# The order of small steps in the output stage of a decoder layer: clamps, powers and PSUM release

## The reference, cut to what matters

```python
z = out.reshape(B, H, S, dh).transpose(0, 2, 1, 3).reshape(B, S, L)
z = z @ Wo
z = _l2_normalize(z)          # z / max(norm(z), 1e-12)
z = z @ Wff
z = _l2_normalize(z)
z = jax.nn.gelu(z, approximate=False)
...
x = _layernorm(x + z)         # (x - mean) / sqrt(var + 1e-5)
```

## Time and profile before

| | us |
|---|---|
| median of 3 runs | 1892.95 (1890.54 to 1895.87) |
| the profiled execution | 1888.5 |
| its span | 1886.7 |
| PE busy in the span | 1778.7 (94%) |
| ACT busy | 1518.7 (80%) |
| DVE busy | 1444.2 (77%) |
| POOL busy | 669.8 (35%) |
| output stage, from its first matmul to the end of the span | 1886.7 - 1808.87 = 77.8 |

### The profile page before, as it was taken

The page is one execution under the profiler, slowest core; times in us unless marked ns, Lnnn a source line. Parts: engine busy times, 40 slices in busy tenths (PEclk is TensorE's granted clock), DMA queues, the critical chain, the costliest instruction groups (busy, mean ns, idle before and its releaser), DMA issues. The chain is left out here.

```text
span 1886.7 us, 42906 instructions
## 1 busy us (share of the span) xinstructions
PE 1778.7 (94%) x16097; PEld 1195.6 (63%) x16198; DVE 1444.2 (77%) x2682; ACT 1518.7 (80%) x4462; POOL 669.8 (35%) x776
## 2 busy tenths in 40 slices
PE   6999999999999999899999989899999999999985
PEld 5888888888888888659999987622222222222232
DVE  6677777777777777456666655699999999999946
ACT  6777777777777777548898855699999999999964
POOL 2343344433333344405675630022222222222222
PEclk9999999999999999999999999999999999999998
DMA  7222323333333332431101006733453353345001
GB/s 179 46 63 63 63 63 60 61 64 63 57 64 63 61 65 54 106 102 41 45 16 44 18 21 163 203 46 46 62 73 46 46 82 54 46 65 71 1 23 67
DMA packets 139773, 121.61 MB, mean 64 GB/s; under 512 B 78876, under 2 KB 111536, under 8 KB 139568
## 3 DMA queue, kind: packets, MB, share of 16 engines
q1 hardware_dynamic: 139567, 118.88, 32.6%
HBM read 77.29 MB, written 41.53 MB: 63 GB/s over the span
## 5 line engine op out<-in xcount | busy, mean ns | idle before, releaser
L1961 DVE TENSOR_REDUCE s_neg_max<-s_ring 128x1 f32<-128x1024 f32 x512 | 580.7, 1295 | 7.0 <-PE s_ring L1879 6.8
L1921 ACT ACTIVATE s_prob<-s_ring,s_neg_max 128x1024 f32<-128x1024 f32 x512 | 569.8, 1114 | 4.1 <-DVE s_neg_max L1961 2.8
L1892 PE MATMUL s_acc<-s_prob,s_v_norm 128*32 128x256 f32 x4096 | 327.4, 393 | 1.9 <-POOL s_v_norm L1944 1.9
L1879 PE MATMUL s_ring<-f_stack 128*128 128x512 bf16 x923 | 288.5, 386 | 27.2 <-issue 17.6
L1940 POOL TENSOR_TENSOR s_row_inv<-s_row_sum,s_neg_one 128x4 f32<-128x4 f32 x128 | 128.8, 1007 | 410.7 <-ACT s_prob L1921 410.7
L1892 PEld LDWEIGHTS s_acc<-s_prob,s_v_norm 128*32 128x32 f32 x4096 | 81.7, 108 | 218.7 <-issue 215.4
L595 POOL TENSOR_SCALAR a_relu_ring<-a_qT 128x512 f32<-128x512 f32 x64 | 98.6, 1557 | 341.8 <-ACT a_qT L463 314.6
L1879 PEld LDWEIGHTS s_ring<-f_stack 128*128 128x128 bf16 x1024 | 58.5, 97 | 232.7 <-ACT s_prob L1921 221.8
L492 ACT ACTIVATE a_prob<-a_psum,a_neg_max 128x128 f32<-128x128 f32 x512 | 179.5, 400 | 21.4 <-DVE a_neg_max L703 21.4
L746 DVE SCALAR_TENSOR_TENSOR a_att<-a_psum,a_keep_cols,a_num_s 128x128 f32<-128x128 f32 x256 | 72.2, 345 | 133.1 <-ACT a_num_s L518 125.9
L1289 ACT ACTIVATE x_prob<-x_psum,x_neg_max 128x77 f32<-128x77 f32 x512 | 160.6, 337 | 14.1 <-DVE x_neg_max L1445 14.1
(11 more groups left out here) (196 smaller groups left out, 4036.8 us busy)
## 6 DMA issues: line engine op xcount, KB each, us to landing
f_stack<-qk_thirds SPq DMA_DIRECT2D x256, 128.0 KB, 7.4
segment_values<-a_v_stage SPq DMA_DIRECT2D x64, 256.0 KB, 3.2
a_v_pos<-segment_values SPq DMA_DIRECT2D x512, 32.0 KB
qk_thirds<-p_third SPq DMA_DIRECT2D x16, 768.0 KB, 7.7
a_x_in<-in_x_dram SPq DMA_DIRECT2D x16, 256.0 KB, 3.4
a_x_res<-in_x_dram SPq DMA_DIRECT2D x32, 128.0 KB, 2.9
after_attention<-a_normed SPq DMA_DIRECT2D x32, 128.0 KB, 2.4
x_x_in<-after_attention SPq DMA_DIRECT2D x32, 128.0 KB, 2.0
```

The lines of the kernel that those rows point to most:

```text
L1879: last = pe.matmul(ring[n % 3][:, f * HALF:(f + 1) * HALF], k_stack[:, slot, j, kt * P:(kt + 1) * P], q_stack[:, slot, j, f * HALF:(f + 1) ...
L1892: last = pe.matmul(acc[32 * j:32 * j + 32, s], v_norm[:, step // KT % 2, step % 4, j, :], prob[:, step % 4, j, s], start=step % (2 * KT) = ...
L1921: act.activation(prob[:, step % 4, j, :], ring[n % 3][:, :], ACT.Exp, bias=neg_max[:, step % 2, j:j + 1], accum_out=row_sum[:, step % 4, j ...
L1961: dve.tensor_reduce(neg_max[:, step % 2, j:j + 1], ring[n % 3][:, :], AX_X, ALU.max, negate=True).then_inc(max_ready, 1)
```

## The change

TensorE now waits by tile, not by step: tile t waits until the gelu of tile t - 8 has signalled, and every gelu signals. The steps are a list of tile counts, `COUNTS` = seven steps of 4 and two of 2, so the last 512 tokens are two steps. Only one tile of squares of step n + 1 stands ahead of the gelus of step n, not two. On VectorE `residual` is cut: it ends after the statistics, and the rest is `variances`. The order in step n becomes residual(n), clamps(n + 1), normalise(n - 1), factors(n + 1), variances(n); at the end stand residual(8), variances(8), normalise(7), normalise(8). On GpSimd norms(n + 1) comes ahead of deviations(n). Slices and semaphore counts follow the tile counts.

```diff
--- before.py
+++ after.py
@@ -1968,8 +1968,12 @@
 def emit_gelu_output(nc, x2_all, zT_all, w_both, out, B, S):
 
     GT = HALF // P
-    STEPS = B * S // HALF
-    PER_BATCH = S // HALF
+    TILES = B * S // P
+    PER_BATCH = S // P
+    COUNTS = [GT] * (TILES // GT - 1) + [GT // 2] * 2
+    STEPS = len(COUNTS)
+    FIRST = [sum(COUNTS[:n]) for n in range(STEPS + 1)]
+    SLOTS = 8
     outf = out.rearrange("b s d -> (b s) d")
     with ExitStack() as ctx:
         def sb(name, shape, dt=F32):
@@ -1978,7 +1982,7 @@
         def sem(name):
             return ctx.enter_context(nc.semaphore("g_" + name))
 
-        psum = ctx.enter_context(nc.psum_tensor("g_psum", [P, 2 * GT, 2 * D], F32))
+        psum = ctx.enter_context(nc.psum_tensor("g_psum", [P, SLOTS, 2 * D], F32))
         neg_half = sb("neg_half", [P, 2 * GT])
         unused = sb("unused", [P, 2, 2, GT, D])
         sums = sb("sums", [P, 2, 2, GT])
@@ -2004,57 +2008,59 @@
             sem("gelu_done"), sem("y_ready"), sem("ln_step"), sem("var_ready"), sem("rstd_ready"), sem("o_ready"))
         stored = [sem("stored0"), sem("stored1")]
 
+        def stores(n):
+            return 16 * sum(COUNTS[m] // 2 for m in range(n % 2, n + 1, 2))
+
         block = ctx.enter_context(nc.Block())
 
         @block.sync
         def _(sp):
             for n in range(STEPS):
-                for half in range(2):
-                    sp.wait_ge(o_ready, 2 * n + half + 1)
-                    first = n * HALF + half * HALF // 2
-                    sp.dma_start(outf[first:first + HALF // 2, :].rearrange("(t p) d -> p t d", p=P),
-                                 o_fin[:, n % 2, half * HALF:(half + 1) * HALF].rearrange("p (t d) -> p t d", d=D)
+                for pair in range(COUNTS[n] // 2):
+                    at = FIRST[n] + 2 * pair
+                    sp.wait_ge(o_ready, at // 2 + 1)
+                    sp.dma_start(outf[at * P:(at + 2) * P, :].rearrange("(t p) d -> p t d", p=P),
+                                 o_fin[:, n % 2, 2 * pair * D:(2 * pair + 2) * D].rearrange("p (t d) -> p t d", d=D)
                                  ).then_inc(stored[n % 2], 16)
-            for parity in range(2):
-                sp.wait_ge(stored[parity], 16 * STEPS)
+            for n in range(STEPS - 2, STEPS):
+                sp.wait_ge(stored[n % 2], stores(n))
 
         @block.tensor
         def _(pe):
-            for n in range(STEPS):
-                if n >= 2:
-                    pe.wait_ge(gelu_done, n - 1)
-                for t in range(GT):
-                    at = n % PER_BATCH * HALF + t * P
-                    for g in range(ZC):
-                        last = pe.matmul(psum[:, n % 2 * GT + t, :], zT_all[:, n // PER_BATCH, g, at:at + P],
-                                         w_both[:, g, :], start=g == 0, stop=g == ZC - 1)
-                    last.then_inc(z_done, 1)
+            for t in range(TILES):
+                if t >= SLOTS:
+                    pe.wait_ge(gelu_done, t - SLOTS + 1)
+                at = t % PER_BATCH * P
+                for g in range(ZC):
+                    last = pe.matmul(psum[:, t % SLOTS, :], zT_all[:, t // PER_BATCH, g, at:at + P], w_both[:, g, :],
+                                     start=g == 0, stop=g == ZC - 1)
+                last.then_inc(z_done, 1)
 
         @block.scalar
         def _(act):
             def squares(n, tiles):
                 for t in tiles:
-                    act.wait_ge(z_done, n * GT + t + 1)
+                    act.wait_ge(z_done, FIRST[n] + t + 1)
                     for k in range(2):
-                        last = act.activation(unused[:, n % 2, k, t, :], psum[:, n % 2 * GT + t, k * D:(k + 1) * D], ACT.Square,
+                        last = act.activation(unused[:, n % 2, k, t, :],
+                                              psum[:, (FIRST[n] + t) % SLOTS, k * D:(k + 1) * D], ACT.Square,
                                               accum_out=sums[:, n % 2, k, t:t + 1])
-                if t == GT - 1:
-                    last.then_inc(squared, 1)
+                    if t == COUNTS[n] - 1:
+                        last.then_inc(squared, 1)
 
             def gelu(n):
                 act.wait_ge(both_ready, n + 1)
                 if n >= 2:
                     act.wait_ge(y_ready, n - 1)
-                for t in range(GT):
-                    last = act.activation(z[:, n % 2, t * D:(t + 1) * D], psum[:, n % 2 * GT + t, D:2 * D], ACT.Gelu,
-                                          scale=both_inv[:, n % 2, t:t + 1])
-                last.then_inc(gelu_done, 1)
-
-            squares(0, range(0, 2))
+                for t in range(COUNTS[n]):
+                    act.activation(z[:, n % 2, t * D:(t + 1) * D], psum[:, (FIRST[n] + t) % SLOTS, D:2 * D], ACT.Gelu,
+                                   scale=both_inv[:, n % 2, t:t + 1]).then_inc(gelu_done, 1)
+
+            squares(0, range(0, 1))
             for n in range(STEPS):
-                squares(n, range(2, GT))
+                squares(n, range(1, COUNTS[n]))
                 if n + 1 < STEPS:
-                    squares(n + 1, range(0, 2))
+                    squares(n + 1, range(0, 1))
                 gelu(n)
 
         @block.gpsimd
@@ -2064,75 +2070,90 @@
 
             def norms(n):
                 pool.wait_ge(clamps_ready, n + 1)
-                pool.tensor_tensor(roots[:, n % 2, :, :].rearrange("p a b -> p (a b)"),
-                                   clamped[:, n % 2, :, :].rearrange("p a b -> p (a b)"), neg_half[:, :], ALU.pow
+                c = COUNTS[n]
+                pool.tensor_tensor(roots[:, n % 2, :, 0:c], clamped[:, n % 2, :, 0:c],
+                                   neg_half[:, 0:2 * c].rearrange("p (a b) -> p a b", a=2), ALU.pow
                                    ).then_inc(roots_ready, 1)
 
             def deviations(n):
                 pool.wait_ge(var_ready, n + 1)
-                pool.tensor_tensor(rstd[:, n % 2, :], var_eps[:, n % 2, :], neg_half[:, 0:GT], ALU.pow
+                c = COUNTS[n]
+                pool.tensor_tensor(rstd[:, n % 2, 0:c], var_eps[:, n % 2, 0:c], neg_half[:, 0:c], ALU.pow
                                    ).then_inc(rstd_ready, 1)
 
+            norms(0)
             for n in range(STEPS):
-                norms(n)
+                if n + 1 < STEPS:
+                    norms(n + 1)
                 deviations(n)
 
         @block.vector
         def _(dve):
             def clamps(n):
...
             def factors(n):
+                c = slice(0, COUNTS[n])
                 dve.wait_ge(roots_ready, n + 1)
...
             def residual(n):
-                dve.wait_ge(gelu_done, n + 1)
-                dve.tensor_tensor(y[:, n % 2, :], z[:, n % 2, :],
-                                  x2_all[:, n * GT:(n + 1) * GT, :].rearrange("p t d -> p (t d)"), ALU.add
+                c = COUNTS[n]
+                dve.wait_ge(gelu_done, FIRST[n] + c)
+                dve.tensor_tensor(y[:, n % 2, 0:c * D], z[:, n % 2, 0:c * D],
+                                  x2_all[:, FIRST[n]:FIRST[n] + c, :].rearrange("p t d -> p (t d)"), ALU.add
                                   ).then_inc(y_ready, 1)
                 dve.wait_ge(y_ready, n + 1)
-                for t in range(GT):
+                for t in range(c):
                     last = dve.bn_stats(stats[:, t, :], y[:, n % 2, t * D:(t + 1) * D])
                 last.then_inc(ln_step, 1)
+
+            def variances(n):
+                c = COUNTS[n]
                 dve.wait_ge(ln_step, 2 * n + 1)
                 dve.memset(spare[:, :], 0.0)
-                for t in range(GT):
+                for t in range(c):
                     last = dve.bn_aggr(mean_var[:, n % 2, t, :], stats[:, t, :])
                 last.then_inc(ln_step, 1)
                 dve.wait_ge(ln_step, 2 * n + 2)
-                dve.tensor_scalar(var_eps[:, n % 2, :], mean_var[:, n % 2, :, 1], LN_EPS, None, ALU.add
+                dve.tensor_scalar(var_eps[:, n % 2, 0:c], mean_var[:, n % 2, 0:c, 1], LN_EPS, None, ALU.add
                                   ).then_inc(var_ready, 1)
 
             def normalise(n):
                 dve.wait_ge(rstd_ready, n + 1)
                 if n >= 2:
-                    dve.wait_ge(stored[n % 2], 32 * (n // 2))
-                for t in range(GT):
+                    dve.wait_ge(stored[n % 2], stores(n - 2))
+                for t in range(COUNTS[n]):
                     s = slice(t * D, (t + 1) * D)
                     last = dve.tensor_scalar(o_fin[:, n % 2, s], y[:, n % 2, s], mean_var[:, n % 2, t, 0:1],
                                              rstd[:, n % 2, t:t + 1], ALU.subtract, ALU.mult)
                     if t % 2 == 1:
                         last.then_inc(o_ready, 1)
 
-            for n in range(STEPS):
-                clamps(n)
+            clamps(0)
+            factors(0)
+            for n in range(STEPS - 1):
+                residual(n)
+                clamps(n + 1)
```

(21 more changed lines are left out.)

## The result

| | before | changed |
|---|---|---|
| median, us (22 runs each) | 1891.8 | 1885.73 |
| ratio to before | | 0.9973 (0.9962 to 0.9983) |
| span of the profiled execution | 1886.7 | 1882.9 |
| output stage: first matmul to the end of the span | 77.8 | 73.2 |

The ratio gives a gain of 0.27% (0.17 to 0.38), about 5.1 us (3.2 to 7.2); the two medians lie 6.1 us apart, which is 0.32%. The direction is clear. On which side of the 0.3% line the gain lies, just past which the forecast had put it, these runs can't tell.

A forecast was written before the change was run, and what follows sets the result against it. The last stage was taken as latency-bound by a circle of waits through ScalarE, VectorE and GpSimd. Start 1.72, loop 4.92 and split 0.0 sum to 6.6 us: 1892.95 to 1886.35 us, range 1883.0 to 1891.0.

The forecast's parts named there:

- 0.3% line: About 0.3% (5.7 us), what a measurement of this kernel can tell from no change; the forecast gain sat just past it.
- Start: Stage start on ScalarE: one tile of squares fewer ahead of the table load and first gelu, gain 1.72 us.
- G(0): Start of the gelus of step 0: 1821.59 before, forecast at 1819.87.
- near 1821: Sign of being wrong at the stage's start: a first gelu near 1821 instead of 1819.9.
- Loop: Circle through ScalarE, VectorE and GpSimd, G(0) to G(6): 6.99 us a step instead of 7.81, 4.92 over six.
- the cover of normalise: VectorE between clamps and product: normalise(n - 1), 1.97, covered by the roots, 2.60; without cover up to 1.3 more.
- Split: Last step in two: 18.3 us from G(6) to the end, as before; 0.9 taken from the rest of the change.
- faster by over 0.3%: Outcome class for the whole kernel's time, given a chance of 0.58; within 0.3% had 0.38, slower 0.04.
- TensorE's pace: Rival in the loop: steps run at TensorE's 6.86 us, gain 7.5, 1885.4 us; chance 0.14.
- satisfied waits on TensorE: Taken at zero; rival, 0.24 a tile lost, 1890.2, within "a part stays away" (also table load waiting, 1887.5), chance 0.18.
- the circle doesn't close elsewhere: Against the no-effect rival: normalise or its store holds the product, old circle length, only start's 1.7 gained, 1891.2; chance 0.05.
- The rule of the Trainium skill: Two-input VectorE and SBUF-reading GpSimd instructions block each other; deviations could hold the big add by 0.1 at most.

The follow-up runs named there:

- PSUM by step: The changed kernel with TensorE waiting once for four gelus, as before, instead of by tile; 1884.81 us in one run.
- two tiles ahead: The changed kernel with eight steps of four tiles (no split) and two tiles of squares ahead of the gelus; 1889.65 us in one run.
- normalise late: The changed kernel with variances(n) between clamps(n + 1) and the product, and normalise(n - 1) behind the product; 1883.36 us in one run.

## Why the prediction was right

By its own steps, at full clock:

- *Start:* forecast G(0) at 11.0 behind the first matmul, gain 1.72. Measured 11.00 with PSUM by step, and 12.7 with two tiles ahead. Right, and so is its reason, the table load that doesn't wait (1821.21, against 1822.13 for the product). The profile of the changed kernel alone would have spoken against it: its first gelus are at 1822.50, 12.80 behind the first matmul, and the forecast's own sign of being wrong was "near 1821", 12.1 behind it. It took the row of the granted clock to tell a slow start from a load that waits.
- *Loop:* forecast 6.99 a step, 4.92 over six; measured 7.00 (6.90 at first), 4.94. The sum is right, but partly by luck, since it hides two errors that nearly cancel: from the last clamp to the norms' power it takes 0.25 in a steady step (1855.17 to 1855.42) and not the 0.32 of the first step, which the forecast had taken; and the power takes 1.75 beside normalise, not 1.64. The step that failed is the cover of normalise: it is covered in its own time, but it holds the power up.
- *TensorE:* forecast no pause, release by tile worth nothing. Both right. So is the pace of 1.716 a tile as the floor: 6.87 a step when the circle is shorter.
- *Split:* forecast 18.3 from step 6 to the end, and 0.9 lost to it. Measured 18.5, and 0.7 lost. The two short powers were taken at 1.01 and took 1.26, so that the steps came to 6.50 and 4.58 and not 6.36 and 4.45; the last piece was 7.4 where 7.5 was forecast. The loss is smaller than forecast because without the split the end is longer than forecast too (17.8 for 17.45), above all by the last power of 1.26.
- *Sum:* 6.6 forecast, 6.4 in the stage (77.8 to 71.4), 5.1 by the ratio of all runs (3.2 to 7.2, which holds both) and 6.1 between the medians. That the median came within 0.6 of 1886.35 is part luck: the 22 runs put before at 1891.8, 1.15 under the 1892.95 from which the forecast started, and the gain between the medians is 0.5 smaller; the two partly cancel.

One figure of its working is off by hundredths and changes nothing: 1886.7 - 1883.63 is 3.07, not 3.05. And the terms that it names for the net gain of a step give 0.70 + 1.01 - 0.93 = 0.78; the 0.82 comes from the start-to-start times.

Its likeliest class, "faster by over 0.3%", stays open: the ratio gives 0.27% and the medians give 0.32%. Between 6.4 and 5.1 stands nothing that these runs can resolve. The low clock at the start of the stage costs 1.6 to 2.2 us where it reaches in, in five of nine profiles of the kernels here, and not in that of before. If it reached in more often in the changed kernel's runs than in those of before, that would account for a difference of this size; one profile each can't tell, and it stays open.

The rivals: TensorE's pace didn't bind by 0.13 a step, and does as soon as the circle is cut further. The table load doesn't wait, satisfied waits on TensorE are free, and the circle doesn't close elsewhere; these three fell by a profile each. The rule of the Trainium skill ("SBUF — State Buffer", Who interferes with whom) was weighed at the wrong place. Where the forecast looked, at a two-input product beside a power, there is no hold-up. The hold-up is at normalise, which takes 0.32 us of VectorE's time per 256 elements and has one tensor input; the section counts such an instruction, outside the two-port modes, as free of contention (which mode it ran in, no row shows). What agrees is its sentence that the order of issue decides: before, the power started 0.07 ahead of normalise and took 1.64, and now it starts 0.16 behind and takes 1.75.

## What to carry to other kernels

Draw the circle of waits that sets a stage's period and add it up from start-to-start times; an operation that leaves it must be weighed against what enters, and against the next floor (here TensorE's pace, only 0.13 us a step below). Splitting the last step pays only when the pieces don't each have to run the whole circle, and when the previous step's leftover work has somewhere to go. And read a stage from its own first instruction: the part ahead of it scattered by 10 us with no change in its code, more than this change is worth.

## What the runs showed of the hardware that wasn't expected

- A GpSimd power that starts 0.16 us after a VectorE `tensor_scalar` (256 columns, pointer scalars, SBUF to SBUF) takes 1.73 to 1.75 us instead of 1.64 (8 columns) and 1.26 instead of 1.01 (4 columns). Started 0.07 us ahead of it, it takes its usual time. The deviations' power of 2 columns takes 0.80 instead of 0.70 behind such an instruction, and that of 4 columns 1.25 to 1.26 instead of 1.01. Aggregations beside a power (normalise late) and a small product (before, at 1865.82) cost nothing.
- TensorE's clock at the start of the stage: it fell to its lower level behind the idle time of 1.95 us at the end of the key softmax, and this reached 3.2 to 4.5 us into the stage in five of nine profiles and not at all in four. Each us of it costs half a us, and ScalarE's circle takes the whole of it over, since nothing in the stage catches up.
